# Attention scores in row tiles: four heads by 512 queries per group, three passes, and one shift per batch

## What is computed

```python
q = (node_features @ Wq).reshape(b, n, h, d).transpose(0, 2, 1, 3)
k = (node_features @ Wk).reshape(b, n, h, d).transpose(0, 2, 1, 3)
scores = jnp.einsum('bhqd,bhkd->bhqk', q, k) / jnp.sqrt(jnp.float32(d))
mask = adjacency_matrix[:, None, :, :] > 0
scores = jnp.where(mask, scores, jnp.float32(-1000000000.0))
w = jax.nn.softmax(scores, axis=-1)
ctx = jnp.einsum('bhqk,bhkd->bhqd', w, v)
...
x = _layernorm(x + _L0_gnn_ref(...), axis=-1)
x = _layernorm(x + _L1_gnn_ref(x, adj, ...), axis=-1)
```

## Time and profile before

| | |
|---|---|
| median of 3 runs | 897.36 us (896.6 to 897.99) |
| profiled execution, its own time | 896.19 us |
| its span, first to last instruction | 894.2 us |
| mean granted clock of PE, share of 2.4 GHz | 0.968 |
| busy: PE, DVE, ACT, POOL | 814.8, 698.0, 701.9, 118.2 us |

### The profile page before, as it was taken

The page is one execution under the profiler, slowest core; times in us unless marked ns, Lnnn a source line. Parts: engine busy times, 40 slices in busy tenths (PEclk is TensorE's granted clock), DMA queues, the critical chain, the costliest instruction groups (busy, mean ns, idle before and its releaser), DMA issues.

```text
span 894.2 us, 19419 instructions
## 1 busy us (share of the span) xinstructions
PE 814.8 (91%) x7597; PEld 398.1 (45%) x7629; DVE 698.0 (78%) x1141; ACT 701.9 (78%) x766; POOL 118.2 (13%) x92
## 2 busy tenths in 40 slices
PE   6299989999999999999999999999999999999681
PEld 3123334334643366334643357334654357434671
DVE  4188779797788977988788977988788987787563
ACT  1299898999679986899779986899769996897050
POOL 4000100030003020031002120122000220122030
PEclk8589999999999999999999999999999999999986
DMA  4647716551266125451365224561364323401001
GB/s 138 151 127 185 152 48 173 150 118 48 83 170 153 48 82 136 130 128 60 107 160 150 47 72 144 152 132 48 113 151 138 63 84 87 92 2 49 1 13 37
DMA packets 51778, 92.14 MB, mean 103 GB/s; under 512 B 3729, under 2 KB 20882, under 8 KB 51666
## 3 DMA queue, kind: packets, MB, share of 16 engines
q1 hardware_dynamic: 51682, 90.85, 39.0%
HBM read 67.63 MB, written 23.20 MB: 102 GB/s over the span
## 4 chain that ended last, share of the span: by engine, by line
PE 67%; ACT 16%; issue 10%; DVE 5%; DMA 0%; POOL 0%; ACTq 0%; POOLq 0%; SPq 0%; DVEq 0%
PE acc L474 17%; ACT weights L619 12%; PE slot L509 12%; PE slot L441 9%; PE slot L450 9%; PE slot L520 3%; PE slot L446 3%; PE slot L453 2%; ACT atts L645 2%; PE slot L557 2%; DVE x L907 2%; PE slot L575 2%; PE slot L567 2%; PE slot L547 2%; PE slot L491 1%
## 5 line engine op out<-in xcount | busy, mean ns | idle before, releaser
L619 ACT ACTIVATE weights<-slot 128x1024 f32<-128x1024 f32 x504 | 491.7, 1041 | 77.3 <-PE slot L450 39.4
L831 DVE SCALAR_TENSOR_TENSOR weights<-mask,weights 128x1024 f32<-128x1024 bf16 x336 | 403.4, 1235 | 53.7 <-ACT weights L619 43.4
L474 PE MATMUL acc<-weights,vst 128*17 128x512 f32 x2048 | 243.3, 593 | 0.0
L441 PE MATMUL slot<-qst,kst 97*32 97x512 bf16 x2240 | 160.5, 383 | 5.8 <-ACT weights L619 5.2
L450 PE MATMUL slot<-qst,kst 97*128 97x512 bf16 x464 | 133.6, 388 | 27.2 <-issue 15.4
L509 PEld LDWEIGHTS slot<-hst,atts 128*128 128x128 f32 x896 | 106.8, 191 | 17.4 <-ACT weights L619 9.6
L509 PE MATMUL slot<-hst,atts 128*128 128x129 f32 x896 | 110.5, 276 | 3.2 <-issue 1.7
L474 PEld LDWEIGHTS acc<-weights,vst 128*17 128x17 f32 x2048 | 52.3, 97 | 119.5 <-issue 96.8
L441 PEld LDWEIGHTS slot<-qst,kst 97*32 97x32 bf16 x2240 | 49.6, 95 | 115.8 <-ACT weights L619 49.3
L846 DVE SCALAR_TENSOR_TENSOR atts<-turn,hst,mask 128x1024 f32<-128x1024 f32 x64 | 83.0, 1321 | 23.2 <-DMA k_scratch<-atts 15.5
L768 POOL TENSOR_TENSOR rstd<-vareps,exponent 128x4 f32<-128x4 f32 (+1 forms) x24 | 29.3, 1221 | 467.0 <-DVE vareps L902 467.0
(11 more groups left out here) (131 smaller groups left out, 676.7 us busy)
## 6 DMA issues: line engine op xcount, KB each, us to landing
raw<-in_adjT SPq DMA_DIRECT2D x64, 512.0 KB, 3.8
q_scratch<-atts SPq DMA_DIRECT2D x48, 256.0 KB
qst<-q_scratch SPq DMA_DIRECT2D x16, 768.0 KB
k_scratch<-atts SPq DMA_DIRECT2D x24, 256.0 KB
kst<-k_scratch SPq DMA_DIRECT2D x16, 384.0 KB
xT_sb<-in_xT SPq DMA_DIRECT2D x8, 512.0 KB, 4.8
kst<-k_scratch SPq DMA_DIRECT2D x16, 256.0 KB
x_sb<-in_x SPq DMA_DIRECT2D x8, 512.0 KB, 4.7
```

Of the source, the lines that this page charges most:

```text
L441: mm = pe.matmul(ps[rows, cols], kst[:, h, keys], qst[:, h, cols], start=True, stop=not by_pe)
L474: mm = pe.matmul(acc[VW * i:VW * i + HD + 1, cols], vst[b % 2][:, t, g * HG + i], weights[:, HG * buffer(b, n) + i, cols], start=(t == 0), ...
L619: act.activation(to, ps[:], ACT.Exp, scale=SCALE).then_inc(exp_done, 1)
L831: dve.scalar_tensor_tensor(out=to, in0=masks[b % 2][:, n % T], scalar=0.0, in1=at, op0=ALU.is_equal, op1=ALU.mult).then_inc(masked, 1)
```

## The change

- A pair of units is made at once. A unit now is two heads by 512 queries by 128 keys, still 128 x 1024 in PSUM. For a pair, PE makes four heads by 512 queries: head i uses the array's rows 32i to 32i+31 (a row tile) and writes a bank of its own. The 32 rows hold two products of parts; three passes accumulate all six. So a pair is 12 matmuls with 32 rows, 128 columns of weights and 512 streamed columns.
- `pair` waits for the slots of both units before its first matmul. `TILED` is gone; masks by PE are always in column tiles.
- The row of shifts is gone, and with it `negshift`, its send and its load. One number per batch takes its place: PE's new job `shift` spreads `widest` over all partitions, DVE makes `unitbias` from it, and the exponential takes it as its bias.
- `q` is sent in four copies instead of six, `k` in six instead of three; a group is loaded by one transfer each of `qst` and `kst` instead of one, three and one.
- `MASKED_BY` has 39 s and 25 m where it had 42 s, 21 m and one d, and the five tables are new.

```diff
-MASKED_BY = ("ssss" "sssm" "ssss" "ssss"
-             "ssmm" "msms" "ssmm" "mssm"
-             "sssm" "smsm" "sssm" "ssmm"
-             "mssm" "ssdm" "mssm" "sssm")
+MASKED_BY = ("smsm" "sssm" "ssss" "smsm"
+             "ssmm" "smsm" "mmss" "sssm"
+             "sssm" "ssss" "smmm" "mmsm"
+             "sssm" "sssm" "smmm" "smss")
...
 ACT_AT = {
-    40: [("exp0", -1)], 45: [("exp1", -1)], 48: [("exp2", -1)], 52: [("exp3", -1)], 54: [("exp4", -1)],
-    60: [("exp5", -1)], 62: [("v0", 1), ("exp6", -1), ("exp7", -1)], 63: [("v1", 1), ("mask0", 1)],
+    0: [("v1", 0), ("exp7", -2)], 1: [("mask1", 0)], 5: [("acc1", -1)], 6: [("mask2", 0)], 9: [("mask3", 0)],
...
+    41: [("exp0", -1)], 43: [("exp1", -1)], 54: [("exp2", -1)], 56: [("exp3", -1)], 58: [("exp4", -1)],
+    60: [("exp5", -1)], 62: [("exp6", -1)], 63: [("v0", 1), ("mask0", 1)],
...
-K_RUNS = ((0, 3), (3, 2), (5, 1))
-Q_COPIES = ((0, 1, 2), (3, 4), (5,))
+Q_COPIES = (((0, 0), (1, 1)), ((1, 0),), ((0, 1),))
+K_COPIES = (((0, 0), (1, 0), (0, 2)), ((0, 1), (1, 1)), ((1, 2),))
...
-            if 0 <= b < batches:
-                uses.append(("unit", b, pos))
+            if 0 <= b < batches and pos % 2 == 0:
+                uses += [("unit", b, pos), ("unit", b, pos + 1)]
...
-        qst = sb("qst", [SROWS, H, N], BF16)
-        kst = sb("kst", [SROWS, H, N], BF16)
+        qst = sb("qst", [128, NG, 2, N], BF16)
+        kst = sb("kst", [128, NG, 3, N], BF16)
...
+            def pair(b, u):
+                n, k = divmod(u, HG)
                 g, t = divmod(n, T)
+                cols = slice(k // 2 * HALF, (k // 2 + 1) * HALF)
+                keys = slice(t * 128, (t + 1) * 128)
...
                 pe.wait_ge(*free_for("unit", b, u))
+                pe.wait_ge(*free_for("unit", b, u + 1))
+                for p in range(3):
+                    for i in range(HG):
+                        rows = slice(VW * i, VW * (i + 1))
+                        to = slot_of("unit", b, u + i // 2)[:, i % 2 * HALF:(i % 2 + 1) * HALF]
+                        by_pe = MASKED_BY[u + i // 2] == "m"
+                        mm = pe.matmul(to, kst[rows, g, p, keys], qst[rows, g, p // 2, cols], start=(p == 0),
+                                       stop=(p == 2 and not by_pe))
+                        if p == 2 and i % 2 == 1 and not by_pe:
+                            mm.then_inc(full["unit"], 1)
+                for j in range(2):
+                    if MASKED_BY[u + j] == "m":
+                        pe.wait_ge(masks_made, b * T + t + 1)
+                        for c in range(2):
+                            for i in range(4):
+                                rows = slice(VW * i, VW * (i + 1))
+                                to = slot_of("unit", b, u + j)[rows, c * HALF:(c + 1) * HALF]
+                                mm = pe.matmul(to, same[:, rows], masks[b % 2][:, t, cols], start=False, stop=True)
+                        mm.then_inc(full["unit"], 1)
...
+                elif name == "shift":
...
+                    mm = pe.matmul(ps[:, 0:2 * VW], widest[:].to_broadcast([2 * VW, 128]), ident[0:2 * VW, 0:2 * VW], **kw)
...
-                act.activation(to, ps[:], ACT.Exp, scale=SCALE).then_inc(exp_done, 1)
+                act.activation(to, ps[:].rearrange("p (h n) -> p h n", h=2), ACT.Exp, bias=unitbias[b % 2][:],
+                               scale=SCALE).then_inc(exp_done, 1)
...
-                link(dve.tensor_scalar(worst[:, B:B + 1], worst[:, B:B + 1], 2.0 * (FARTHEST - EXPONENT / SCALE / 2.0), None, ALU.add))
+                link(dve.tensor_scalar(worst[:, B:B + 1], worst[:, B:B + 1], -1.0, 2.0 * FARTHEST, ALU.mult, ALU.add))
```

More of the change, by code:

```diff
@@ L129, in build_fast @@
     WIDEST = X1_NORM * ((1.0 - ALPHA) ** 2 + (1.0 + ALPHA) ** 2) ** 0.5
-    STACK_DMAS = 5
+    STACK_DMAS = 2
+    Q_DMAS = sum(len(to) for to in Q_COPIES)
+    K_DMAS = sum(len(to) for to in K_COPIES)
     SUMS = 2 * VW + 1
@@ L174, in build_fast @@
         masks = [sb(f"mask{i}", [128, T, N], BF16) for i in range(2)]
-        qst = sb("qst", [SROWS, H, N], BF16)
-        kst = sb("kst", [SROWS, H, N], BF16)
+        qst = sb("qst", [128, NG, 2, N], BF16)
+        kst = sb("kst", [128, NG, 3, N], BF16)
         vst = [sb(f"vst{i}", [128, T, H, HD + 1], F32) for i in range(2)]
         weights = sb("weights", [128, 3 * HG, N], F32)
-        negshift = sb("negshift", [H, N], BF16)
         widest = sb("widest", [2 * VW, 1], F32)
-        negkmax = sb("negkmax", [H, 1], F32)
-        worst = sb("worst", [H, B + 1], F32)
+        highest = sb("highest", [128, 2], F32)
+        unitbias = [sb(f"unitbias{i}", [128, 1], F32) for i in range(2)]
+        worst = sb("worst", [128, B + 1], F32)
         too_far = sb("too_far", [128, 1], I32)
@@ L307, in buffer, with weights_of @@
             return (b * QUADS + n) % 3
+        def weights_of(b, u):
+            n, k = divmod(u, HG)
+            first = HG * buffer(b, n) + k % 2 * 2
+            return weights[:, first:first + 2, k // 2 * HALF:(k // 2 + 1) * HALF]
         block = ctx.enter_context(nc.Block())
@@ L340, in send_parts @@
                 for i in range(3):
-                    for to in [q_scratch[:, r] for r in Q_COPIES[i]] if s == 0 else [k_scratch[:, i]]:
-                        sp.dma_start(to, parts[s][i]).then_inc(parts_out[s], 16)
-            def send_shift(b):
-                if b > 0:
-                    for g in range(NG):
-                        sp.wait_ge(stack_in[g], b * 16 * STACK_DMAS)
-                sp.wait_ge(taken["cc"], b + 1)
-                sp.dma_start(shift_scratch, negshift[:]).then_inc(shift_out, 16)
+                    for r, a in (Q_COPIES, K_COPIES)[s][i]:
+                        sp.dma_start((q_scratch, k_scratch)[s][:, r, :, a], parts[s][i]).then_inc(parts_out[s], 16)
             def load_stack(b, g, what):
@@ L384, in job @@
                     send_parts(me, "qk".index(name[5]))
-                elif name == "shift":
-                    send_shift(me)
                 else:
@@ L431, in unit @@
                 pe.wait_ge(*free_for("unit", b, u))
-                by_pe = MASKED_BY[u] == "m"
-                if by_pe:
-                    pe.wait_ge(masks_made, b * T + t + 1)
-                if TILED[u] == "t":
-                    for c in range(2):
-                        cols = slice(c * HALF, (c + 1) * HALF)
-                        for i in range(4):
-                            rows = slice(VW * i, VW * (i + 1))
-                            keys = slice(t * 128 + VW * i, t * 128 + VW * (i + 1))
-                            mm = pe.matmul(ps[rows, cols], kst[:, h, keys], qst[:, h, cols], start=True, stop=not by_pe)
-                    for c in range(2 if by_pe else 0):
-                        cols = slice(c * HALF, (c + 1) * HALF)
-                        for i in range(4):
-                            rows = slice(VW * i, VW * (i + 1))
-                            mm = pe.matmul(ps[rows, cols], same[:, rows], masks[b % 2][:, t, cols], start=False, stop=True)
-                else:
-                    for c in range(2):
-                        cols = slice(c * HALF, (c + 1) * HALF)
-                        mm = pe.matmul(ps[:, cols], kst[:, h, t * 128:(t + 1) * 128], qst[:, h, cols], start=True, stop=not by_pe)
-                    for c in range(2 if by_pe else 0):
-                        cols = slice(c * HALF, (c + 1) * HALF)
-                        mm = pe.matmul(ps[:, cols], same[:], masks[b % 2][:, t, cols], start=False, stop=True)
@@ L454, in unit @@
-                mm.then_inc(full["unit"], 1)
+                pe.wait_ge(*free_for("unit", b, u + 1))
[8 more added lines that the diff above has]
+                            mm.then_inc(full["unit"], 1)
@@ L592, in _ @@
                 for pos in range(UNITS):
-                    if 0 <= b < B:
-                        unit(b, pos)
+                    if 0 <= b < B and pos % 2 == 0:
+                        pair(b, pos)
                     if at := context_at(b, pos, B):
@@ L665, in job @@
                     return
-                if name == "cc":
-                    act.wait_ge(kmax_made, me + 1)
-                    act.wait_ge(shift_out, me * 16)
-                    ins = act.activation(negshift[:], ps[0:H], ACT.Identity, bias=negkmax[:], scale=-1.0)
-                elif name in ("v0", "v1"):
+                if name in ("v0", "v1"):
                     tt = slice(4 * int(name[1]), 4 * int(name[1]) + 4)
@@ L723, in _ @@
                         job(name, me)
-                        if me == 0 and name == "cc":
+                        if me == 0 and name == "k":
                             copy_folded()
@@ L753, in _ @@
                                pattern=[[-1, 128]], channel_multiplier=1)
-            pool.memset(half[:], 0.5)
             pool.memset(cutoff[:], BIG / 2.0)
@@ L829, in mask_unit @@
                         dve.wait_ge(contexts_done, b * QUADS + n - 2)
-                    at = slot_of("unit", b, u)[:]
```

(4 more changed lines are left out.)

83 lines of the change are left out of this document (40 added, 43 removed), and 36 rows, old and new, of tables (ACT_AT, DVE_AT, PE_AT, SP_AT).

## The result

The changed kernel takes 1009.1 us (median of 4 runs, 1001.67 to 1012.83), beside 896.98 us for the kernel before on the same chip. The ratio is 1.125, with a 95% interval of 1.1187 to 1.1313. The forecast was 927 us, 880 to 962: the sign was right and the size far off.

A forecast was written before the change was run, and what follows sets the result against it. PE was taken to bound a batch's first 78 us, ACT with DVE close behind the other 24.1. Profiled 896.2 - 7 (PE work) + 37 (slot waits) = 926, so 927 us by the runs' median; range 880 to 962.

The forecast's parts named there:

- The score passes: Scores on PE: four row tiles run side by side, 0.215 us a pass, 0.645 a pair; -55 us.
- rival 2: Row tiles run only partly side by side, a pass taking 0.24 us: about 948 us; chance 0.17.
- change of form: On PE, matmuls following another form take 0.11 us longer; 300 more such changes, +33 us.
- Work on PE: PE's scores, added masks, changes of form and new shift matmul together: -55 + 14 + 33 + 1 = -7 us.
- The ring of three slots: Pairs wait for two score slots, 1.95 us pair to pair; those with little work behind lose time: +37 us.
- short gaps: Ten pairs a batch with only a mask (two masks in "mm") or nothing behind them: 7.4 us short together.
- second stretch: Last 24.1 us of a batch, ended by ACT: 2.7 us of waits cancel against about -1.9, taken as 0.
- single waits: Before, each unit waited for one slot, so PE ran ahead and only ACT's rate counted, at most 0.96 us a unit.
- The exponential: On ACT, 1.02 us each in the slot loop, as before; no term for its new bias.
- The six sends of k: Mid-batch: DVE's second-layer sum moves three positions (about 5 us) later, for three more one-microsecond issues: no term.
- Rival 1: Slot waits are not on the path, only work counts: 875 us, up to 890; chance 0.27.
- Rival 3: Effects cancel, half the switches hidden (-16) and slot waits half absorbed (-18): 893 to 897 us; chance 0.04.

The follow-up runs named there:

- a_early: Changed kernel without the exponential's bias, the three sends of k's first part moved from position 31 to 26: 973.8 us.
- b_tables: Scores, shift, transfers and exponential of the kernel before, in the changed kernel's order and masks, pairs waiting for both slots: 998.3 us.
- b_noshift: Kernel before without any shift (no 97th row, no negshift, none of its transfers): 896.8 us.
- b_tables_own: As b_tables, scores of before in the changed order and masks, in pairs, but each unit waits for its own slot alone: 972.0 us.
- b_tables_single: Kernel before, unit by unit with single waits, but with the changed kernel's MASKED_BY and tables: 990.8 us.
- b_pairs: Kernel before with units made two at a time in PE's order, each waiting for its own slot: 1024.4 us.
- a_nobias: Changed kernel with the exponential's bias operand left out; all that makes the shift still runs: 991.3 us.
- b_bias: Kernel before with a bias operand of zeros in the exponential: 916.4 us.
- a_contig: Changed kernel with each unit's weights written in one run of 1024 instead of two of 512: 1003.9 us.
- a_split: Changed kernel without the exponential's bias, each context cut in two halves, one behind every pair: 962.2 us.
- a_spread: Changed kernel without bias, contexts split, k sent early, with k, x1T, cc, h0 and their readers mostly one to four positions later: 998.6 us.
- b_pairs_wait2: Kernel before with units made two at a time in PE's order, each pair waiting for both slots: 1087.9 us.

## Why the prediction was right in sign and wrong in size

**The score passes: right.** 0.76 us a pair before other work, forecast 0.645 + 0.11. Four row tiles do run side by side here, and rival 2 is out: at the 0.28 us that the Trainium skill's 3.07 gives, an estimate, a pair would have taken 0.95 us with its change of form. Here the trace does not agree with "TensorE: Matmul & The Clock Gate", Part 3 (measured speedup), of the Trainium skill; in a steady row of passes the four tiles cost one stream.

**Work on PE: the balance fits, in part by luck.** a_early and b_tables differ in the form of the scores, and in the shift's and q's transfers, whose price before was nothing (b_noshift) or small. They lie 24.5 us apart in favour of row tiles, on one chip. The forecast had -55 + 33 = -22. Neither kernel has a bias operand, and a_early has its k sent early, so this is the gain with the two side costs kept out. The count of changes of form fits too (576 in the trace after, 296 in b_tables). But both kernels wait on PE, PE's busy time differs by 37.9 us (814.8 and 852.7), and the granted clock was 0.970 in the one and 0.957 in the other, so that the two figures meet doesn't prove the terms. Against the kernel before, PE's busy time grew by 17.6 us where -7 was forecast. 6.2 of that lie behind the last exponential, at the lower clock. More of it is how busy time is counted: a group of mask matmuls counts 0.61 us when a wait follows and 0.44 when a context does. The rest is not taken apart.

**The ring of three slots: the step that failed.** The forecast priced it at +37: "So a pair with a context, an output or another job behind it loses nothing", and only the ten pairs of the short gaps counted, of which four were taken as free in the second stretch. (The ten shortages add up to 7.3 us a batch and not 7.4; it changes nothing.) The loop was right to 0.17 us (2.12 against 1.95). The batch shown above, position by position, tells where the price went wrong:
- Behind the ten pairs PE waits 9.3 us, where 7.3 was forecast: 0.75 us instead of 0.65 behind most (1.13 at 406.14), 1.17 and 1.24 instead of 0.73 behind the two "mm". The four in the second stretch are 3.5 us of it.
- In other places it waits some 5 us, where the forecast had none. A job also takes a slot, whose reader must be done before a wait for that slot ends. The pair at 411.98 shows it (0.75 us, x1T), as do v1's copy (1.1 us, `vst` in the list of waits), the matmuls of v0 (L521, 1.1) and the pair behind `fi` and h1 (at 433.67 us, 1.0 for an exponential). The forecast adds up the work behind a pair and forgets who has to free what that work used.
- In all PE is idle for 14.8 us of the batch, where it was 2.5. The 12.3 more are 98 us in eight batches, where the forecast had 37.

The forecast's "single waits" argument named only the wait for two slots, which is worth 26 us in the new order (b_tables less b_tables_own) and 63 in the old. Why b_tables_own is still 75 us behind the kernel before is argued, not shown. Units made one by one let the three engines be one or two units apart, and this lead may have absorbed the jobs. But the new order costs 94 us without any pair (b_tables_single), so what belongs to the grouping and what to an order that fits it less well was not parted. b_pairs doesn't part them either.

**The exponential, priced as unchanged: wrong by 13 to 20 us.** No term of the sum had its bias. a_nobias and b_bias agree, from both ends: +18 (12.6 against a_contig, which ran on its chip) and +20 us. The row was there to read: the activation L645 has a bias operand, and in the earlier trace rows the next instruction starts 1.04 us after it, while three exponentials without one last 2.88. I even used that 1.04 for the second layer. (L645 reads SBUF and not a slot, so the row is a hint and no proof.) The Trainium skill has it too, "ScalarE: Activation LUTs", What ACT_TABLE_LOAD costs: about 93 ns for each pointer operand. The runs agree: 91 ns in b_bias, 89 between the changed kernel and a_nobias.

**The six sends of k, "no term": wrong by up to 18 us.** The forecast set a delay of three positions against three microseconds of issue. It did not ask when the last send lands, 12.3 us after the first issue in a_nobias. With three sends in the new order there is no such wait (b_tables). DVE waited 21.8 us in all in the changed kernel, 15.5 before, but now up to 4.3 us at a time instead of 3.4. a_early takes it away and gains 17.5 us alone, 7 on top of a_split.

**The start: right. The second stretch and the tail: priced at nothing, and longer.** The first exponential starts at 41.2 us, where it started at 42.5. From the exponential of position 48 to the next batch's first it takes 24.7 us, where it took 22.9: 1.8 us a batch. Without the bias it is 23.5 (a_nobias), so most of it is the bias. The larger part of a batch's loss lies in its first 48 positions: 79.3 us before, 90.9 to 93.6 after in five batches from the third on. The tail grew by 8.5 us in the profiled execution, by 3.5 in that of a_contig.

**The rivals.** Rival 1 (the slots are not waited for on the path) fell with its own test: short-gap pairs start 2.12 us apart, not under 1.8. Rival 3 fell with the time. (The forecast's own 927 + 50 for rival 2 is 977 and not 970.)

**What stays open.** Without the bias, with early sends and split contexts the kernel is at 955 us, 28 over the forecast. Its pairs still wait 43.7 us for exponentials, but which part of them a better table would fill was tried in one direction alone (a_spread), and that failed. Whether a fourth slot would bring the row tiles' 24 us home was not tried. None of the fifteen kernels beats the one before; b_noshift ties with it.

## What to carry to other kernels

Before work is fused into larger pieces, ask how many pieces the ring of buffers holds: with three slots, units of two leave no whole piece in reserve. List every user of a slot, jobs too, and ask of each who frees it and when. A table tuned by hand belongs to one grouping: run the new grouping in the old order (b_pairs) and the new order with the old grouping (b_tables_single). Here each alone cost more than the two together (127 and 94 us against 75). When an instruction gets one operand more, look for the nearest row with that operand and multiply by its count: here 512 times 0.09 us, 46 us of the engine's time, of which the kernel paid less than half.

## What the hardware showed that I had not expected

- A bias from SBUF lengthens a 128 x 1024 exponential by 89 to 91 ns (1026 to 1115, 1041 to 1132), whether it is zero or not.
- Behind three waits of 1.13, 0.75 and 1.29 us PE is at 1.2 GHz for a few microseconds (granted 0.50 in 414 to 416 us): 16 context matmuls took 2.84 us instead of 1.91. It isn't a rule: behind the same three waits the clock fell in three batches of six. In b_pairs_wait2, where PE waits more, the mean of 600 us is 0.94, where the kernel before has 1.00.
- From the end of the releasing exponential to the first matmul of a pair it takes 0.14 us in the short gap shown, where 0.05 was read from the rows of before. Why it is longer was not tried.
